# A three-part transformer kernel: the inverse deviation of one norm moves from GpSimd to ScalarE, and the written-out order of most steps is renewed

## What is computed

```python
x = x + mamba(LN(x))          # selective scan: conv, silu, softplus, h = exp(d*A)*h + d*x*b
x = ffn(LN(x)) + x            # "call 1": two layers, below
x = x + power(LN(x))          # attention with |S|^2 scores and a decay, 16 heads of 8
x = ffn(LN(x)) + x            # "call 2": the same two layers

def layer(x):                 # feed-forward part, 8 heads of 64, window 64
    q, k, v = heads(shift(x) @ wqkv)
    q, k = rotary(l2norm(q) * qs, l2norm(k) * ksc)
    x = x + local_attention(q, k, v) @ wo
    h = shift(x)
    h = (h - mean(h)) / sqrt(var(h) + 1e-5) * lg + lb
    a, g = split(h @ w1 + b1)
    return x + (a * gelu(g)) @ w2 + b2
```

## Time and profile before

| | |
|---|---|
| median of 3 runs | 3021.56 us (3019.85 to 3024.13) |
| the profiled execution | 3025.83 us, span 3024.0 us |
| TensorE busy | 2689.8 us (89%), 18848 matmuls |
| VectorE busy | 2430.5 us (80%) |
| ScalarE busy | 2222.0 us (73%) |
| GpSimd busy | 1390.7 us (46%) |
| mean granted TensorE clock | 0.975 of full |

### The profile page before, as it was taken

One profiled execution on the slowest core, in us unless ns is written; L12 is line 12 of the kernel. 1 busy time (PEld: TensorE's weight loads), 2 busy tenths in 40 slices (PEclk: granted clock), 3 DMA queues, 4 the chain that ended last, 5 costly groups with the idle time before them and its releaser, 6 DMA issues. The chain is left out here.

```text
span 3024.0 us, 55902 instructions
## 1 busy us (share of the span) xinstructions
PE 2689.8 (89%) x18848; PEld 1827.4 (60%) x18848; DVE 2430.5 (80%) x3798; ACT 2222.0 (73%) x5986; POOL 1390.7 (46%) x1217
## 2 busy tenths in 40 slices
PE   6788988789999999999899999996899999999997
PEld 3454454356666666666677777774566666666665
DVE  7999999877777777777788888887777777777774
ACT  5688788467677677667699999994676776677674
POOL 5767777665555455545410000004555455555542
PEclk8999999899999999999999999998999999999998
DMA  3000000000000000000000000000000000000000
GB/s 93 1 1 1 1 1 1 1 1 1 2 1 1 12 13 1 1 1 1 12 13 2 2 2 2 2 2 1 1 1 1 1 1 13 16 6 5 7 7 6
DMA packets 15670, 17.83 MB, mean 6 GB/s; under 512 B 3837, under 2 KB 12862, under 8 KB 15294
## 3 DMA queue, kind: packets, MB, share of 16 engines
q1 hardware_dynamic: 13616, 12.30, 1.3%
q10 hardware_dynamic: 1774, 1.95, 0.3%
HBM read 12.16 MB, written 2.10 MB: 5 GB/s over the span
## 5 line engine op out<-in xcount | busy, mean ns | idle before, releaser
L1058 POOL TENSOR_TENSOR f_p<-f_p,f_rs 128x512 f32<-128x512 f32 (+1 forms) x256 | 321.1, 1254 | 697.9 <-DVE f_rs L1007 697.9
L901 ACT ACTIVATE f_p<-pair,f_nm 128x128 f32<-128x128 f32 (+1 forms) x1024 | 389.7, 392 | 190.0 <-DVE f_nm L996 189.3
L1050 POOL TENSOR_TENSOR f_qb<-f_kn,f_tab 128x512 f32<-128x512 f32 x256 | 441.4, 1746 | 149.6 <-DVE f_kn L975 149.6
L679 POOL TENSOR_TENSOR m_hc<-m_h,m_c 128x512 f32<-128x512 f32 x256 | 322.5, 1281 | 152.3 <-DVE m_h L646 114.0
L646 DVE TENSOR_TENSOR_SCAN m_h<-m_a,pair 128x1024 f32<-128x1024 f32 x128 | 292.2, 2283 | 11.8 <-ACT m_a L608 1.7
L855 PE MATMUL bank<-f_hnT,f_w 128*128 128x256 f32 (+1 forms) x768 | 212.6, 400 | 83.1 <-DVE f_u L1033 81.5
L608 ACT ACTIVATE m_a<-m_delta,m_A 128x255 f32<-128x255 f32 x512 | 217.3, 496 | 62.3 <-DVE m_h L646 61.7
L767 PE MATMUL pair<-f_wqkv,f_hT 128*128 128x512 f32 x512 | 253.6, 618 | 8.5 <-DVE f_kn L975 7.0
L815 PE MATMUL pair<-ident,f_p 128*128 128x128 f32 x1536 | 246.5, 284 | 14.9 <-POOL f_p L1058 6.9
L965 DVE TENSOR_REDUCE f_ss<-f_sq 128x16 f32<-128x1024 f32 x128 | 155.3, 1213 | 127.3 <-ACT f_sq L872 127.3
L533 PE MATMUL bank<-m_hc,ident 128*128 128x512 f32 x512 | 248.6, 620 | 0.0
(11 more groups left out here) (179 smaller groups left out, 6557.8 us busy)
## 6 DMA issues: line engine op xcount, KB each, us to landing
f_wqkv<-in_f_wqkv SPq DMA_DIRECT2D x4, 768.0 KB, 4.0
out_x<-X SPq DMA_DIRECT2D x16, 128.0 KB, 1.8
f_w<-in_f_w SPq DMA_DIRECT2D x4, 341.0 KB, 3.4
f_wo<-in_f_wo SPq DMA_DIRECT2D x4, 256.0 KB, 2.7
sel<-in_sel ACTq DMA_DIRECT2D x1, 768.0 KB
f_w<-in_f_w SPq DMA_DIRECT2D x4, 192.0 KB, 3.3
m_taps<-in_m_taps ACTq DMA_DIRECT2D x1, 512.0 KB, 4.9
X<-in_x SPq DMA_DIRECT2D x1, 512.0 KB, 9.1
```

The costliest lines, as they stand in the source:

```text
L679: op = nc.gpsimd.tensor_tensor(m_hc[:, g % 4, n], m_h[:, g % 2, n], m_c[:, g % 2, n].unsqueeze(1).broadcast_to([P, EC, L]), ALU.mult)
L901: op = nc.scalar.activation(f_p[:, t, j, k0:k1], SC[:, j, k0:k1], ACT.Exp, bias=f_nm[:, t, j:j + 1], accum_out=f_sm[:, t, j:j + 1])
L1050: op = nc.gpsimd.tensor_tensor(f_qb[:, t, :, o].rearrange("p (x h) d -> p x h d", x=2), f_kn[:, t, :, 32 - 32 * e:64 - 32 * e].rearrange(" ...
L1058: op = nc.gpsimd.tensor_tensor(f_p[:, t, :, k0:k1], f_p[:, t, :, k0:k1], f_rs[:, t, :].unsqueeze(2).broadcast_to([P, 4, k1 - k0]), ALU.mult)
```

## The change

1. The steps vv and rv of a feed-forward item leave GpSimd. ScalarE gets rl (Ln of the variance, with eps as its bias) and rv (Exp with scale -0.5). hn waits for ScalarE's rv.
2. `F_STAGES`, `F_ORDER`, `P_STAGES`, `P_ORDER`, `START`, `MF`, `FP` and `PF` are new. `M_ORDER` is not changed. In the feed-forward rounds T11, o01 and pT110 of TensorE and p11, pe010, Te10, oe0, Te11 and pe110 of ScalarE now stand at the head of the next round's list; in the cycle of rounds most of them keep their neighbours.
3. `span` can put norm steps beside the steps of a round: in the feed-forward rounds of call 1's layer two (st, mv, z, ve, rs for the power part) and in the power rounds (st, mv, z, ve, rs, xb for call 2). Those norms leave `FP` and `PF`, except the last ones. Call 2 and layer one of call 1 have none beside them.
4. The loads of `m_first` and `m_last` are issued by SP, after the first and after the third part of x. ScalarE issues none.
5. TensorE begins with ten matmuls of `ones` into pair[2], and the memsets of GpSimd are split in two steps.

```diff
 F_ORDER = {
-    "dve": "hT nm00 pe111 ss0 rs00 cl0 nm10 kn0 z1 qa0 rs10 st nm01 mv qs0 hn ss1 cl1 rs01 pe101 kn1 nm11 qa1 u1 "
-        "qs1 u0 rs11 z2",
-    "pe": "xT s00 pT111 qk0 o11 s10 wo pT000 v0 sh s01 qk1 o00 v1 s11 pT100 T00 hnT pT101 T01 w1a o10 pT010 w1b w1c "
-        "o01 T10 w2 T11 pT110",
-    "act": "sq0 oe1 lr0 rn0 p10 hb pe000 ve0 p01 sq1 ve1 pe100 Te00 he lr1 rn1 g0 oe0 pe010 Te01 g1 p11 Te10 Te11 "
-        "pe110 p00",
-    "pool": "pn00 qb0 vv rv pn10 pn01 qb1 zb pn11"}
+    "dve": "hT nm00 pe111 rs00 ss0 cl0 nm10 kn0 z1 qa0 rs10 st mv nm01 ss1 hn cl1 qs0 rs01 kn1 qa1 nm11 u1 pe101 "
+        "qs1 u0 rs11 z2",
+    "pe": "T11 o01 pT110 xT s00 pT111 qk0 o11 s10 wo v0 qk1 sh s01 pT000 v1 pT100 hnT s11 w1a o00 T00 w1b T01 pT101 "
+        "w1c pT010 o10 T10 w2",
+    "act": "p11 pe010 Te10 oe0 Te11 pe110 p00 sq0 oe1 lr0 rn0 p10 ve0 hb sq1 pe000 rl rv p01 lr1 ve1 rn1 he g0 pe100 "
+        "Te00 g1 Te01",
+    "pool": "pn00 pn10 qb0 pn01 qb1 pn11 zb"}
...
 P_ORDER = {
+    "dve": "rm10 lg cum hg pe02 he hi r1 vc u11 pe03 mid m11 mid2 rm11 u12 lo pe10 m12 ot0 rm12 pe11 kc0 u13 kc1 "
+        "m13 rm13 pe12 u00 m00 rm00 pe13 u01 ot1 m01 rm01 rn0 u02 y0 m02 u03 m03 rm02 rn1 rm03 y1 pe00 u10 m10 "
+        "pe01 min",
...
+P_BESIDE = {"dve": [("kc0", "mv", 4), ("rm13", "z", 4), ("pe00", "st", 3)],
+            "pool": [("", "ve", 4), ("", "rs", 4), ("", "xb", 4)]}
+F_BESIDE = {"dve": [("z2", "st", 2), ("pe111", "mv", 3), ("rs11", "z", 3)],
+            "pool": [("pn01", "ve", 3), ("pn01", "rs", 3)]}
 
-def span(eng, ph, first, last, base=0):
+def span(eng, ph, first, last, base=0, beside={}, use=0, count=0):
     for k in range(first, last + 1):
-        yield from window(eng, ph, k, base)
+        mine = [(at, ("n", s, use * NSEQ + k - back - count)) for at, s, back in beside.get(eng, []) if k - back > count]
+        yield from (n for at, n in mine if at == "")
+        for item in window(eng, ph, k, base):
+            yield item
+            yield from (n for at, n in mine if at == item[1])
...
+            elif s == "rl":
+                act.wait_ge(*dve_f.at(i, "mv"))
+                op = nc.scalar.activation(f_ve[:], f_mv[:, :, 1], ACT.Ln, bias=eps[:, 0:1])
+            elif s == "rv":
+                act.wait_ge(*act_f.at(i, "rl"))
+                op = nc.scalar.activation(f_rv[:], f_ve[:], ACT.Exp, scale=-0.5)
...
             elif s == "mv":
                 dve.wait_ge(*dve_f.at(i, "st"))
-                dve.wait_ge(*pool_f.at(i - 1, "vv"))
+                dve.wait_ge(*act_f.at(i - 1, "rl"))
             elif s == "hn":
-                dve.wait_ge(*pool_f.at(i, "rv"))
+                dve.wait_ge(*act_f.at(i, "rv"))
...
-            elif s == "vv":
-                pool.wait_ge(*dve_f.at(i, "mv"))
-                op = nc.gpsimd.tensor_tensor(f_ve[:], f_mv[:, :, 1], eps[:, 0:T], ALU.add)
-            elif s == "rv":
-                pool.wait_ge(*pool_f.at(i, "vv"))
-                op = nc.gpsimd.tensor_tensor(f_rv[:], f_ve[:], mhalf[:, 0:T], ALU.pow)
...
+                if n == 0:
+                    for t, name in m_first:
+                        sp.dma_start(t, ins[name]).then_inc(m_first_loaded, 16)
+                if n == 2:
+                    for t, name in m_last:
+                        sp.dma_start(t, ins[name]).then_inc(m_last_loaded, 16)
...
+                if ph == "c":
+                    pe.wait_ge(small_set, SMALL)
+                    for _ in range(10):
+                        nc.tensor.matmul(pair[2][:, 0:L], ones[:, 0:P], ones[:], start=True, stop=True)
...
-            for t, name in m_first:
-                act.dma_start(t, ins[name]).then_inc(m_first_loaded, 16)
-            for t, name in m_last:
-                act.dma_start(t, ins[name]).then_inc(m_last_loaded, 16)
```

More of the change, by code:

```diff
@@ L84 @@
     "xT hT qk0 v0 sq0 ve0 v1 ve1 ss0 cl0 lr0 rn0 kn0 qa0 qb0 qs0 qk1 sq1 ss1 cl1 lr1 rn1 kn1 qa1 qb1 qs1 "
[4 rows of a table removed]
[5 rows of a table added]
 F_ORDER = {
-    "dve": "hT nm00 pe111 ss0 rs00 cl0 nm10 kn0 z1 qa0 rs10 st nm01 mv qs0 hn ss1 cl1 rs01 pe101 kn1 nm11 qa1 u1 "
+    "dve": "hT nm00 pe111 rs00 ss0 cl0 nm10 kn0 z1 qa0 rs10 st mv nm01 ss1 hn cl1 qs0 rs01 kn1 qa1 nm11 u1 pe101 "
         "qs1 u0 rs11 z2",
-    "pe": "xT s00 pT111 qk0 o11 s10 wo pT000 v0 sh s01 qk1 o00 v1 s11 pT100 T00 hnT pT101 T01 w1a o10 pT010 w1b w1c "
-        "o01 T10 w2 T11 pT110",
-    "act": "sq0 oe1 lr0 rn0 p10 hb pe000 ve0 p01 sq1 ve1 pe100 Te00 he lr1 rn1 g0 oe0 pe010 Te01 g1 p11 Te10 Te11 "
-        "pe110 p00",
-    "pool": "pn00 qb0 vv rv pn10 pn01 qb1 zb pn11"}
-P_STAGES = [
[6 rows of a table removed]
-P_ORDER = {
[7 rows of a table removed]
+    "pe": "T11 o01 pT110 xT s00 pT111 qk0 o11 s10 wo v0 qk1 sh s01 pT000 v1 pT100 hnT s11 w1a o00 T00 w1b T01 pT101 "
[3 more added lines that the diff above has]
+    "pool": "pn00 pn10 qb0 pn01 qb1 pn11 zb"}
+P_STAGES = [
+    "xT xTe g abs min exp ln hgT v",
[5 rows of a table added]
+P_ORDER = {
[7 rows of a table added]
     "pool": "x"}
@@ L260, in program @@
     yield from join(eng, MF[eng], {"n": NSEQ})
-    yield from span(eng, "f", MF_F + 1, FP_F - 1)
+    yield from span(eng, "f", MF_F + 1, FP_F - 1, 0, F_BESIDE, 2, NSEQ)
     yield from join(eng, FP[eng], {"n": 2 * NSEQ})
-    yield from span(eng, "p", FP_P + 1, PF_P - 1)
+    yield from span(eng, "p", FP_P + 1, PF_P - 1, 0, P_BESIDE, 3)
     yield from join(eng, PF[eng], {"n": 3 * NSEQ, "f": 2 * NSEQ})
@@ L1340, in _ @@
             xv = ins["x"].rearrange("b (t p) d -> p b t d", p=P)
-            for (a, e), part in zip(X_PARTS, x_loaded):
+            for n, ((a, e), part) in enumerate(zip(X_PARTS, x_loaded)):
                 sp.dma_start(X[:, a:e, :].rearrange("p b (t d) -> p b t d", t=T), xv[:, a:e]).then_inc(part, 16)
+                if n == 0:
[4 more added lines that the diff above has]
+                        sp.dma_start(t, ins[name]).then_inc(m_last_loaded, 16)
             for t, name in consts:
@@ L1371, in step @@
             def step(ph, s, i):
-                if ph == "m":
+                if ph == "c":
+                    pe.wait_ge(small_set, SMALL)
+                    for _ in range(10):
+                        nc.tensor.matmul(pair[2][:, 0:L], ones[:, 0:P], ones[:], start=True, stop=True)
+                elif ph == "m":
                     m_pe(pe, s, i, i % 2)
@@ L1450, in first @@
                     pool.wait_ge(small_set, SMALL)
-                elif s == "wide":
+                elif s == "wide_f":
                     nc.gpsimd.memset(f_hT[:, 0:1], 0.0).then_inc(wide_set, 1)
                     nc.gpsimd.memset(f_p[:], 0.0).then_inc(wide_set, 1)
+                elif s == "wide_p":
                     nc.gpsimd.memset(p_v[:, :, :, :, 0:PS + 1].rearrange("p b t h d -> p (b t) h d"),
```

## The result

The changed kernel takes 2875.64 us (median of 4 runs, 2874.79 to 2876.04), the kernel before 3021.62 beside it: a ratio of 0.9516, 95% interval 0.9499 to 0.9532. The forecast was 2923, the range 2880 to 2992.

A forecast was written before the change was run, and what follows sets the result against it. It took steady feed-forward rounds as bound by TensorE plus about 2 us of stalls, power rounds by ScalarE. Rounds -66, rounds beside norms -15.4, start -7, joints -10 sum to -98.4: 2927 profiled, 2923 as median; range 2880 to 2992.

The forecast's parts named there:

- The walk: Steady feed-forward round followed step by step through the new lists, with step lengths from the old round's timelines; 26.5 us.
- The joint into call 2: Stretch between power and call 2: most norms leave it for the power rounds; 5 us less, bounds 0 and 15.
- The start: Issues on SP let ScalarE's table load and xe come sooner; net 7 us less, bounds -14 and +3.
- The round: Steady feed-forward round, xT to xT: 28.0 us becomes 26.5, minus 1.5; bounds 25.9 and 28.9.
- Beside norms: Last 14 steady rounds of call 1: norms add 0.4 us, giving 26.9; bounds 0 and 1.5.
- The number of rounds: Feed-forward calls: about 58 steady rounds priced, 44 at -1.5 us and 14 at -1.1.
- Power: 14 power rounds, bound by ScalarE with unchanged work: no change, bounds -1.0 and +1.0 us a round.
- The diagnosis: Old steady round: u1's string makes TensorE wait before w1c; hn is late, waiting 0.87 us for GpSimd's rv.
- TensorE bound: Steady rounds: the walk's waits vanish and TensorE alone bounds them at 25.9 us; 2883 us, chance 0.12.
- One lock on the string: Steady rounds: hn behind qb0's second half, or qs1 behind late qb1, about 0.8 us; 2969 us, chance 0.21.
- The other side: Steady rounds: qb0 shuts out both hn and qs0; rounds of 28.9 us, 3057 us, chance 0.07.
- Table loads: ScalarE: a table load comes with rl or rv, 2 x 1.28 us; about 3068 us, counted with The other side.

The follow-up runs named there:

- e8: The changed kernel with the weights of the scan part loaded from ScalarE again instead of SP; 2873.83 us.
- e7: The changed kernel with unmerged joints on both sides of power and the power lists of the kernel before; 2916.76 us.
- e1: The changed kernel with all its new lists, but vv and rv on GpSimd again, between qb0 and pn01; 2929.82 us.
- e2: The kernel before with its old lists, only the inverse deviation moved from GpSimd to ScalarE (rl, rv between ve0 and p01); 3012.06 us.
- e3: The changed kernel with qb0 ahead of pn10 again on GpSimd in the repeated feed-forward rounds; 2874.42 us.
- e11: The changed kernel with hn ahead of ss1 on VectorE and rl, rv ahead of pe000 on ScalarE in the steady feed-forward rounds; 2910.41 us.
- e9: The changed kernel with vv and rv back on GpSimd, ahead of qb0 in its list; 2995.16 us.
- e4: The changed kernel with a second Ln and a second Exp of two columns beside rl and rv, into an unused tile; 2887.61 us.
- e12: e11 with he directly behind p01, ve1 behind g0, Te00 behind g1, and TensorE's w1b ahead of T00, w1c ahead of T01; 2944.62 us.

## Why the prediction was off

**What held.** The walk's order of events is that of the trace, and most of its times are within 0.3 us: kn0 6.85 (6.91 in the walk), sh 10.05 (10.30), hb 10.86 (11.12), rv done 13.3 (13.46), hn 13.8 (13.97), hnT 14.46 behind 0.79 of wait (14.60, 0.85), w1a 16.13 (16.45), T10 22.7 (23.1), xT 26.13 (26.45 to 26.65). hn 0.34 each, qa0 1.22, no third table load, rl 0.29 and rv 0.20 (0.22 each): nearly as written. The joint into call 2 was -3.9 for -5.

**What came out by luck.** The start was -8.3 for -7, but not by the working. xe did start sooner (11.41 us for 14.14; the forecast said near 10) and took 3.72 us instead of 6.33, yet m_skip and ue held VectorE, and at the second item of the scan only 1.4 us were gained. The rest came by the sixth item, in the merged rounds of `START`, and e8, with the loads back on ScalarE, gains 5.5 us there too. Which of the new lists does it no run shows.

**What failed.** Three terms of the sum.
- The round: 26.5 was 26.14. The step is "each step as long as it is in the old round's timelines": TensorE's steps came out shorter under the new order. From qk1 to sh the walk gave 1.92 us, which took 1.72, and it had w1c wait 0.2 to 0.4 us, which it does not. So the bound of 25.9 for TensorE's busy time was none either: it fell to 25.2. On 44 rounds this is 16 us. Beside norms 26.9 was 26.33, 8 us: the norms cost 0.19 us and not 0.4. The two z's take 1.72 us beside pn11, but are done 0.7 us before z2 can start; what is left shows at w2, behind a u0 that qs1 and qb1 push.
- The number of rounds: I priced 29 in each call, of 34. The other ten stand in the joints and the tail, where I had put 0, -5 and 0; at -1.86 each they are worth 19 us, and the joint into call 1, the one into power and the tail were 5.8 + 5.3 + 5.7 = 16.8 us better than forecast. That the one is the other is worked out, not shown by a run, and the joint into call 2 speaks against it in part: its first three rounds are 6.9 us shorter from xT to xT, the joint as a whole only 3.9.
- Power, taken as 0 within bounds of 1.0 either way, was -0.73 a round, -9.4 (for 13 steady rounds; the 14 of the prediction were one too many). ScalarE's idle time of 1.0 us was in the rows; I left it because I did not follow the power lists as I had followed the others. e7 shows that the lists do it.

16 + 8 + 17 + 9 are the 50 us between -98.4 and -150.4, but for 2.

**The diagnosis.** "What makes it late is on VectorE: hn waits for rv" was wrong for the kernel before, though the forecast did not suffer. hn did wait, but no one waited for hn: the row of hnT, which stood in the timeline that I had read and which I passed over, has no idle time before it. The gain comes first from the new lists (1.20 of 1.86 us, e1), and the lock and the power's place decide only then. That of the lists it is hnT's new place that takes away the waiting is argued from the timelines, not shown. A forecast for e2 alone, made by the prediction's reading, would have been wrong by most of its size; the expectation of e2 above is such a one. The port's lock itself is as the Trainium skill has it (SBUF — State Buffer, "SBUF: two separate sides": a shared port pair held exclusively), and the trace agrees: qa0 2.18 beside qb0 and 1.22 alone. What e3 and e11 add is when it costs: nothing where VectorE would have idled, and everything queued behind it where it would not.

**The rivals.** TensorE bound (25.9, 2883 us): its time is nearer to the measured one than mine, by luck; TensorE is busy 25.2 of 26.14, so the waits did not vanish, and 0.79 is one. One lock on the string: not in the changed kernel, but e9 shows it at 1.24 us a round and e11 at 0.59; e1's 0.66 is a queue (vv behind qb0), with hn at 0.60 us and no lock on it. The other side: qb0 ahead of hn is e9, and it did not come above before. Table loads: none.

## What to carry to other kernels

Before an instruction is called late, look at the row of the one that consumes it: idle time before the producer is worth nothing if the consumer shows none. Where a round is a ring, measure from one fixed point of it to the round's end in several variants: where that distance holds, what moves the point moves the round by nearly as much, and where it does not (e4, e11, e12), something behind the point is late. A busy time that was read under one order is no floor under another. Count the rounds in the joints too, and walk every list that a change touches, the one behind an engine at 97% as well.

## What the hardware showed that I had not expected

- A second tiny pair of ACTIVATEs of two columns costs 0.28 us in all: instructions of 0.29 and 0.20 us overlap with their neighbours by some 0.1 each.
- The lock's price moves instead of going: freed of vv and rv, GpSimd started pn10 0.15 us ahead of qs0 and made that 2.40 us (e2).
- In e9, where TensorE waited 2.15 us in every feed-forward round, 22 of them ran at a granted clock of 0.94 or lower and 1.6 us longer or more; in the changed kernel, with a wait of 0.79 us, none did.
- On GpSimd the same two instructions took 0.19 and 0.70 us with the port free (e1), where vv had taken 1.17.
